# Graph attention layer on one core: mask tiles as the stationary operand, W-projected features (258 columns) moving, five row groups of 6, 7, 8, 7 and 4 tiles

## The reference

```python
# x: (4096, 128) f32, adj: (4096, 4096) int32 (0 or 1), sparse
h = jnp.maximum(_layernorm(x), 0.0)            # relu of the normalised rows
H = h @ W_fc + b_fc                            # 4096 x 128
scores = (H @ w_att[:d])[:, None] + (H @ w_att[d:])[None, :] + b_att
scores = where(adj > 0, scores, -1e9)
out = x + softmax(scores, axis=1) @ H
```

## Time and profile before

| | us |
|---|---|
| median of three runs | 186.04 (185.82 to 186.31) |
| the profiled execution | 186.24 |
| its span (first to last instruction) | 184.3 |
| outside the span | 1.94 |
| PE busy | 160.3 |
| DVE busy | 124.9 |
| ACT busy | 79.6 |
| mean DMA rate | 389 GB/s |

### The profile page before, as it was taken

The page is one execution under the profiler, slowest core; times in us unless marked ns, Lnnn a source line. Parts: engine busy times, 40 slices in busy tenths (PEclk is TensorE's granted clock), DMA queues, the critical chain, the costliest instruction groups (busy, mean ns, idle before and its releaser), DMA issues.

```text
span 184.3 us, 2691 instructions
## 1 busy us (share of the span) xinstructions
PE 160.3 (87%) x866; PEld 115.3 (63%) x866; DVE 124.9 (68%) x360; ACT 79.6 (43%) x232; POOL 10.7 (6%) x33
## 2 busy tenths in 40 slices
PE   0639859989499999989899999999999998999970
PEld 0326638666386867656668667686786775887750
DVE  0995696947999556788865569496594624459931
ACT  2567894999395052222251422442224424021020
POOL 2103601000130020000000000000000000000000
PEclk9999987999969999999999999999999999999995
DMA  5999999999999999999999999999999999998212
GB/s 144 410 439 432 412 443 420 434 420 430 427 430 432 412 441 411 441 420 428 420 422 424 427 427 424 422 427 423 425 424 427 437 431 427 411 398 329 76 60 59
DMA packets 8369, 71.63 MB, mean 389 GB/s; under 512 B 929, under 2 KB 1698, under 8 KB 3490
## 3 DMA queue, kind: packets, MB, share of 16 engines
q1 hardware_dynamic: 7776, 71.18, 92.3%
q10 hardware_dynamic: 578, 0.26, 0.5%
HBM read 69.34 MB, written 2.10 MB: 388 GB/s over the span
## 4 chain that ended last, share of the span: by engine, by line
DMA 59%; PE 23%; DVE 10%; issue 2%; ACT 2%; SPq 1%; DVEq 0%
DMA ring<-adj 59%; PE bank L844 9%; PE bank L850 8%; DVE mask L514 5%; PE bank L868 3%; PE bank L892 2%; PE bank L882 1%; DVE low L537 1%; ACT mask L456 1%; DVE mask L523 1%; ACT weighted L363 1%; SPq L271 1%; DVE x_sb L639 1%; DVE x_sb L646 1%; SPq L277 0%
## 5 line engine op out<-in xcount | busy, mean ns | idle before, releaser
L514 DVE TENSOR_SCALAR mask<-ring 128x1024 fp32r<-128x1024 int32 (+2 forms) x69 | 63.1, 934 | 41.6 <-DMA ring<-adj 37.1
L844 PE MATMUL bank<-mask,high 128*128 128x512 f32 x256 | 80.7, 418 | 11.0 <-DVE mask L514 6.3
L850 PE MATMUL bank<-mask,low 128*128 128x512 f32 x256 | 76.3, 401 | 0.0
L844 PEld LDWEIGHTS bank<-mask,high 128*128 128x128 f32 x256 | 47.8, 196 | 31.1 <-DVE mask L514 12.9
L850 PEld LDWEIGHTS bank<-mask,low 128*128 128x128 f32 x256 | 49.8, 194 | 11.1
L456 ACT ACTIVATE mask<-ring,half_steep 128x512 fp32r<-128x512 int32 x43 | 28.9, 718 | 62.1 <-DMA ring<-adj 60.6
L868 PE MATMUL bank<-mask,w_cols 128*32 128x512 bf16 x256 | 19.7, 392 | 2.3 <-ACT lines L422 2.3
L868 PEld LDWEIGHTS bank<-mask,w_cols 128*32 128x32 bf16 x256 | 5.9, 94 | 13.1 <-issue 8.7
L363 ACT ACTIVATE weighted<-relu,w_over_std 128x128 f32<-128x128 f32 x32 | 10.1, 391 | 4.7 <-DVE w_over_std L608 4.5
L374 ACT ACTIVATE relu<-x_sb,neg_mean 128x128 f32<-128x128 f32 x32 | 9.8, 388 | 3.2 <-DVE neg_mean L546 3.2
L389 ACT ACTIVATE high<-x_sb,neg_mean 128x128 fp32r<-128x128 f32 x24 | 9.3, 387 | 0.0
(11 more groups left out here) (85 smaller groups left out, 67.7 us busy)
## 6 DMA issues: line engine op xcount, KB each, us to landing
ring<-adj SPq DMA_DIRECT2D x18, 2048.0 KB, 17.1
ring<-adj SPq DMA_DIRECT2D x16, 1536.0 KB, 12.9
ring<-adj SPq DMA_DIRECT2D x3, 1024.0 KB, 9.3
out<-x_sb SPq DMA_DIRECT2D x7, 256.0 KB, 13.8
x_sb<-x SPq DMA_DIRECT2D x1, 1024.0 KB, 20.7
ring<-adj SPq DMA_DIRECT2D x4, 256.0 KB, 16.2
x_sb<-x SPq DMA_DIRECT2D x2, 256.0 KB, 3.8
x_sb<-x SPq DMA_DIRECT2D x1, 512.0 KB, 10.1
```

The source lines that it names most:

```text
L514: nc.vector.tensor_scalar(mask[:, n % MASKS, 0:cols], ring[:, n // 2 % RING, begin:begin + cols], 0.0, None, ALU.is_gt).then_inc(masks_rea ...
L844: nc.tensor.matmul(bank[:, b, :], high[:, t, :], mask[:, n % MASKS, cols], start=(t == 0), stop=False)
L850: last = nc.tensor.matmul(bank[:, b, :], low[:, t, :], mask[:, n % MASKS, cols], start=False, stop=(t == T - 1))
```

## The change

The operands of the large product change places. The mask is now the stationary operand, 128 source nodes by 128 destination rows, and the moving one is a row of 258 columns for each source tile: the high part of the W-projected weighted features (128), the high part of w_j (1), and the low parts of both (129). A PSUM bank gathers, for one tile of 128 destination rows, features and denominator together. There are 32 x 32 = 1024 such matmuls. The denominator matmuls, the turning of denominators into columns, the products by W at a group's end and POOL's splitting of w_j in three are gone.

W is applied ahead of time instead: for each chunk of four source tiles PE transposes relu (`turn`), ACT copies it out (`take_turned`), PE multiplies by W (`features_of`), and `weigh` reads the result in PSUM. There is one PSUM bank for the transposes and one for the features.

A group is now as many row tiles as it has banks: 6, 7, 8, 7, 4. A unit is two source tiles by 768 to 1024 rows (four by 512 in the last group). Group 0 has 16 units, 8 pairs and 12.6 MB. `MASKS` falls from 6 to 4, and a mask is freed by its own unit (`units_done`, at a group's end `sums_done`). The last pair of units of a group, and the first of the next, run bank by bank (`by_rows`), so that banks become free one after another. All tiles get their statistics by BN_STATS on DVE. At a group's end ACT copies the banks out (258 columns each), and DVE adds the high and the low part in separate instructions (`add_sums`), then the mean (`add_means`). In the last group DVE reads the banks.

```diff
-GROUPS = [(0, 4), (4, 3), (7, 1)]
+GROUPS = [(0, 6), (6, 7), (13, 8), (21, 7), (28, 4)]
-MASKS = 6
+MASKS = 4
+    WIDE = 2 * (D + 1)
...
+            def take_turned(c):
+                act.wait_ge(turned, c + 1)
+                if c >= 2:
+                    act.wait_ge(features_in_psum, c - 1)
+                nc.scalar.copy(relu_T[:, c % 2, :], ps_turned).then_inc(relu_T_ready, 1)
             def weigh(u):
                 t0, t1 = SPLITS[u]
+                act.wait_ge(features_in_psum, t0 // PER + 1)
...
-                    last = nc.scalar.activation(weighted[:, u % 2, at], relu[:, t, :], ACT.Copy, scale=w_over_std[:, t:t + 1])
+                    last = nc.scalar.activation(weighted[:, u % 2, at], ps_features[:, of], ACT.Copy, scale=w_over_std[:, t:t + 1])
...
+            def add_sums(g, tiles):
+                r0, width = GROUPS[g]
+                for part in range(2):
+                    of = slice(part * (D + 1), part * (D + 1) + D)
+                    for b in tiles:
+                        row = r0 + b
+                        source = sums[:, b, of] if g < LAST_GROUP else bank[:, BANKS[g][b], of]
+                        last = nc.vector.scalar_tensor_tensor(out=x_sb[:, row, :], in0=source, scalar=inv_den[:, row:row + 1],
+                                                              in1=x_sb[:, row, :], op0=ALU.mult, op1=ALU.add)
...
+            def turn(c):
+                pe.wait_ge(relu_ready, PER * c + PER)
...
+                for q in range(PER):
+                    last = nc.tensor.transpose(ps_turned[:, q * P:(q + 1) * P], relu[:, PER * c + q, :], ident[:])
+                last.then_inc(turned, 1)
+            def features_of(c):
+                pe.wait_ge(relu_T_ready, c + 1)
...
+                    pe.wait_ge(weighted_ready, split_of(PER * c - 1) + 1)
+                for q in range(PER):
+                    last = nc.tensor.matmul(ps_features[:, q * D:(q + 1) * D], relu_T[:, c % 2, q * P:(q + 1) * P], w_sb[:],
+                                            start=True, stop=True)
+                last.then_inc(features_in_psum, 1)
+            def sum_of(n, i, b):
+                g, t0, _ = UNITS[n]
+                width = GROUPS[g][1]
+                t = t0 + i
+                if t == 0 and copies_before(g, b) > 0:
+                    pe.wait_ge(sums_copied, copies_before(g, b))
...
+                at = (i * width + b) * P
+                last = nc.tensor.matmul(bank[:, BANKS[g][b], 0:WIDE], mask[:, n % MASKS, at:at + P],
+                                        features[:, t, :, :].rearrange("p h d -> p (h d)"), start=(t == 0), stop=(t == T - 1))
```

More of the change, by code:

```diff
@@ L257, in unit_landed, with mask_free @@
                 engine.wait_ge(pair_landed[pair % RING], 16 * (pair // RING + (pair % RING > 0)))
+        def mask_free(engine, n):
+            before = n - MASKS
+            if closes(before):
+                engine.wait_ge(sums_done, tiles_before(UNITS[before][0] + 1))
+            else:
+                engine.wait_ge(units_done, sum(not closes(m) for m in range(before + 1)))
         block = ctx.enter_context(nc.Block())
@@ new lines, in add_means @@
+            def add_means(g, tiles, done):
+                r0, width = GROUPS[g]
+                if g < LAST_GROUP:
+                    dve.wait_ge(sums_read, g + 1)
+                for b in tiles:
+                    row = r0 + b
+                    last = nc.vector.scalar_tensor_tensor(out=x_sb[:, row, :], in0=mean_H[:], scalar=is_empty[:, row:row + 1],
+                                                          in1=x_sb[:, row, :], op0=ALU.mult, op1=ALU.add)
+                    if done is last_results_ready or b == width - 1:
@@ L688, in _ @@
+            row_weights(2)
+            for t in range(20, 24):
+                stats_of(t)
+            mask_unit(5)
+            split(4)
+            for t in range(24, 32):
+                last = stats_of(t)
+            link(last)
+            link(sum_of_halves(2))
+            negative_mean(2).then_inc(means_ready, 1)
+            split(5)
+            mask_unit(6)
             deviations(2, between_2)
[L689 removed]
+            for t in range(28, 32):
                 last = dot_of(t)
@@ new lines, in by_tiles @@
+            def by_tiles(n):
+                g, t0, step = UNITS[n]
+                masks_of(n)
+                for i in range(step):
+                    if g == 0 and t0 + i in [s[0] for s in SPLITS]:
+                        u = split_of(t0 + i)
+                        pe.wait_ge(w_parts_ready, STAGE_OF[t0 + i] + 1)
+                        pe.wait_ge(high_ready, u + 1)
+                        pe.wait_ge(low_ready, u + 1)
+                    for b in ORDERS[g]:
+                        last = sum_of(n, i, b)
+                last.then_inc(units_done, 1)
```

636 lines of the change are left out of this document (280 added, 356 removed).

## The result

The changed kernel takes 209.75 us (median of 4 runs, 207.97 to 211.52), the kernel before 185.93 beside it: ratio 1.1194, 95% interval 1.1162 to 1.1225. Forecast were 200 us and 189 to 208: right in sign and in the place of the loss, too low in its size.

What follows compares the result with a forecast made beforehand. The adjacency stream through the DMA engines was taken to bound the kernel: last landing 168.3, plus 15.4 of empty queue, 12.9 of tail, 1.4 for the clock and 1.94 around the span gave 200 us, range 189 to 208.

Steps and rivals of the forecast that it cites:

- DVE until the mask of unit 7: First stage on DVE: start, work and added statistics and masks sum to 39.0; with waits and its own mask, done at 42.0.
- pair 1 (0.8), pair 2 (0.5) and ACT (0.8): DVE's forecast waits before unit 7's mask, for two stream pairs and for ACT; they raise 39.0 to 41.1.
- The chain from there to unit 13: PE, ACT and DVE in turn from unit 7's mask to unit 13's: 21.1 us, done at 63.1.
- Clock: PE at 1.2 GHz after its wait before unit 7: up to 2.8 us, half taken, 1.4; bounds 0 and 5.
- 15.4 us of empty queue: DMA stream: pair 10 lands at 69.2, not 53.8; the last piece moves from 168.3 to 183.7.
- The tail: From the last landing to the span's end: 12.9 us where it was 16.0, a gain of 3.1.
- The price of a pair: PE's weight load plus 258 columns: 0.118 us, bounds 0.099 and about 0.21; 1024 pairs take 121 us under the stream.
- the first (only DVE's own work counts, 189.7): First stage: ACT and PE keep up, no chain forms, pair 7 lands at 47.5; 189.7 us, chance 0.15.
- The second (the first stage fits, 183.1): First stage: masks are ready in time and the tail's gain stays; 183.1 us, faster, chance 0.05.
- The third (loads show): PE: weight loads show or the clock stays low; about 205 us at 0.15 a pair, 251 at 0.21; chance 0.10.
- the main case: Whole kernel: the forecast of 200 us, 14 slower, range 194 to 206, chance 0.70.

Runs made afterwards that it cites:

- experiment 2: Changed kernel with the identity loaded by a 64 KB DMA on ACT's queue instead of POOL's memset and affine_select: 203.5 us (200.59 to 203.82).
- experiment 1: Changed kernel with ACT, not POOL, copying a_wide, so it does not stand behind the identity: 207.46 us, ratio 1.1123.
- experiment 3: Kernel before with only POOL's identity moved ahead of a_wide: 186.43 us against 185.80, ratio 1.0033.
- experiment 7: Kernel of experiment 2 plus 13 f32 products that nothing reads, in PE's wait ahead of unit 7: 199.39 us, ratio 1.0728.
- experiment 5: Kernel of experiment 2 with row weights computed earlier on ACT and chunks turned and features computed earlier on PE, by order alone: 195.66 us, ratio 1.0499.
- experiment 4: Changed kernel, identity by DMA, with statistics, scores and features of tiles 8 to 31 left out (tiles 0 to 7 reused): 184.03 us, ratio 0.9898.

## Why the prediction was wrong

By its own steps, in the order of the sum:

- *"DVE until the mask of unit 7"*, done at 42.0. **This is the step that failed**, by 5.7 us. Its work sum holds: 39.0 less the first 4.3 is 34.7, and up to unit 7's mask at 46.73 DVE's timeline has 34.1 outside its waits. With the identity out of the way the mask is done at 40.2 (experiment 2), within 2 us of the forecast. What failed is the list of waits, "pair 1 (0.8), pair 2 (0.5) and ACT (0.8)", 2.1 in all. Neither wait for a pair came; the waits were 6.56 for `v_rows` and 2.11 for `w_j`, 8.7 in all, 6.6 more than listed. A few lines of the change move the identity on POOL ahead of `a_wide`; the prediction costs them at nothing, by not naming them. They put the 6.56 us ahead of DVE's first score. The row with the 10.99 us stood in the trace of before, where nobody waited for it. Taking the identity off POOL gives 7.4 us at unit 7 and 4.5 at the last issue (experiment 2 against the changed kernel); freeing only one of its two users gives little (experiment 1); the move alone costs the kernel before 0.6 (experiment 3).
- *The chain from there to unit 13*, 21.1: right. 22.5 in the changed kernel with the clock's share in it, 21.1 with PE at 2.4 GHz (experiment 7), and shorter when the order of issue is changed (experiment 5). That it fits to the tenth is luck: between chunk 4's split and units 8 and 9 the sum left out chunk 5's products and the turning of chunk 6, 0.7 in experiment 7 (the split is done at 46.7, unit 8 starts at 47.4), and terms slightly too large elsewhere make up for it.
- *Clock*, 1.4 with bounds 0 and 5: right for the changed kernel. Against the same instructions in experiment 7 unit 7 takes 2.95 and not 1.70 and the turning of chunk 4 0.79 and not 0.60, 1.4 together. That the half of 2.8 fits is luck, since nothing was worked out for it. In the kernel of experiment 2 it is 25.5 - 21.1 = 4.4, within the bounds. Why the 1.2 GHz lasted until 52 us in the one and only into the turning of chunk 4 in the other, after waits of 4.46 and 4.14 us, these runs don't settle.
- *"15.4 us of empty queue, which nothing gives back, as the rest of the stream runs at the DMA's pace"*: the pace is right, the size 2.0 short. By the forecast's own count pair 10 lands 6.1 behind unit 13's mask, at 76.3, 22.5 later than the 53.8 without a stall; the last issue moves by 24.5. What the two kernels had moved by these two times (windows, first of before, then of the changed kernel):

```profile
0.00:53.80 53.80, 37.90 (x166) 26.66 (x167) 39.29 (x164) 39.62 (x167) 9.72 (x32) 0.94 0.98 403
```

```profile
0.00:76.30 76.30, 46.23 (x303) 42.05 (x304) 48.34 (x216) 33.33 (x95) 1.20 (x9) 0.96 0.70 268
76.30:175.90 99.60, 86.41 (x674) 83.15 (x674) 76.77 (x179) 30.96 (x52) 0.50 (x1) 0.98 1.01 427
```

  From 76.3 on the stream runs at 427 GB/s, so nothing more is lost there. But 403 x 53.8 is 21.7 MB and 268 x 76.3 is 20.5: the stream is 1.2 MB, or 2.9 us, further behind than the landing of one pair tells. At the last issue the changed kernel has moved 0.3 MB less than before, which takes 0.7 of it off; 2.2 are left, the 2.0 within the rounding. The bytes missing from the whole queue (25.0 us, above) tell the cost of the stall better than the landing of one pair does.
- *The tail*, 3.1 gained: 2.6 in the changed kernel, 2.75 in experiment 4, both counted from the last issue. Right to 0.5.
- *The price of a pair*, 0.118: right. PE's timeline of the changed kernel, two stretches at 2.4 GHz:

```profile
56.21 3.12 PE L867 MATMUL bank<-features,mask 128*128 128x258 f32 x24
...
60.42 1.69 PE L867 MATMUL bank<-features,mask 128*128 128x258 f32 x12
```

  12 more pairs take 1.43 us more, 0.119 each, and the 0.26 left over is the drain (forecast 0.25). The Trainium skill, "TensorE: Matmul & The Clock Gate", section "What overlaps and what doesn't", has the loads of one row group not overlap, by which a pair would be the sum, about 0.21. The traces of all kernels here disagree: PE's weight loads are busy for 144.1 us of the changed kernel beside 152.5 us of matmuls, in a span of 206.2.

With the failed step put right, 16.8 + 5.7 + 2.0 = 24.5, and 184.3 + 24.5 - 2.6 + 1.8 is the profiled execution, 207.97 but for rounding.

Of the rivals, the first (only DVE's own work counts, 189.7) fell: the chain costs what the forecast says, though experiment 5 shows how much of it was the order on PE and ACT. The second (the first stage fits, 183.1) is what experiment 4 builds, and it measured 184.03. The third (loads show) fell. The range ended 1.75 us short of the median and just above the profiled 207.97. That it came so close is luck too, since its top of 208 was made from the third rival; the main case was given 194 to 206 and had no room for a wait that nobody had listed.

## What to carry to other kernels

When a change makes something an early input, look up when it is made now, on every engine, the slow and idle ones first: a row that reads "10.99 <-issue" costs nothing until someone stands behind it. Work out the slack of a stage before moving work into it; the same move cost 0.6 us with 79 us of stream to hide in, and 4.6 to 7.6 with 29. And where a chain goes back and forth between engines, the cheapest cures here were order (4.9 to 7.7 us) and keeping PE's clock up across the wait (1.2 to 4.0; the two overlap, 5.7 to 8.5 together), while moving work to an engine that looks less busy lost 7.0.

## What the runs showed of the hardware

- POOL idles for 10.99 us ahead of its only affine_select in before and in the changed kernel, from 5.5 us as from 1.1 us of the span, for 11.59 in experiment 1 and for 12.90 in experiment 3; the instruction itself takes 0.28. A DMA of the same 64 KB landed 4.4 us after its issue (in the kernel of experiment 5, among three other small ones).
- 26 matmuls that nothing reads, 3.06 us in a wait of 4.46, brought the granted clock of the stretch from 40 to 50 us from 0.50 to 1.00, and the time down by 1.2 to 4.0 us.
- ScalarE takes 0.68 us a tile for mean and variance in two accumulating passes, VectorE 0.21 with BN_STATS.
